# The first folds of a gated feed-forward kernel: factors in two halves, folds ahead of the first product, one low part moved to GpSimd

## What is computed

```python
xn = layernorm(x)                                   # over the 512 columns
def lora_linear(x, w, a, b):                        # a has rank 16
    return x @ w.T + (x @ a.T) @ b.T * 2.0
h = silu(lora_linear(xn, w1, A1, B1)) * lora_linear(xn, w3, A3, B3)    # 1376 hidden units
g = silu(lora_linear(h, w2, A2, B2))
s = causal_convolution(xn, K) + D * xn              # K: an S4 kernel of 512 taps
out = x + s * g
```

## Time and profile before

| | us |
|---|---|
| median of 3 runs (406.47 to 406.7) | 406.63 |
| the profiled execution | 406.52 |
| its span in the trace | 404.7 |
| TensorE busy in the span | 399.2 (99%) |
| VectorE busy | 207.4 (51%) |
| ScalarE busy | 111.5 (28%) |
| GpSimd busy | 80.3 (20%) |

### The profile page before, as it was taken

The page is one execution under the profiler, slowest core; times in us unless marked ns, Lnnn a source line. Parts: engine busy times, 40 slices in busy tenths (PEclk is TensorE's granted clock), DMA queues, the critical chain, the costliest instruction groups (busy, mean ns, idle before and its releaser), DMA issues.

```text
span 404.7 us, 5106 instructions
## 1 busy us (share of the span) xinstructions
PE 399.2 (99%) x1838; PEld 332.9 (82%) x1838; DVE 207.4 (51%) x323; ACT 111.5 (28%) x185; POOL 80.3 (20%) x141
## 2 busy tenths in 40 slices
PE   8999999999999999999999999999999999999996
PEld 7988888888888888888888888888888888888885
DVE  5877776794883336553345236754236134411227
ACT  7554232222541111222232112222123111211122
POOL 6686745403510113300000101600000000000000
PEclk9999999999999999999999999999999999999999
DMA  8583743614325102000005301000002000000002
GB/s 275 147 218 97 230 149 110 209 41 126 110 89 173 52 2 52 2 1 0 2 1 193 118 0 52 0 0 0 0 0 104 2 0 0 2 0 0 2 0 104
DMA packets 14515, 26.90 MB, mean 66 GB/s; under 512 B 2816, under 2 KB 4576, under 8 KB 14368
## 3 DMA queue, kind: packets, MB, share of 16 engines
q1 hardware_dynamic: 13488, 24.53, 19.1%
q0 software_dynamic: 720, 1.60, 1.5%
q10 hardware_dynamic: 288, 0.52, 0.3%
HBM read 21.45 MB, written 4.54 MB: 64 GB/s over the span
## 4 chain that ended last, share of the span: by engine, by line
PE 95%; DVE 1%; DMA 1%; ACT 1%; issue 1%; POOL 0%; DVEq 0%; ACTq 0%; POOLq 0%
PE h L1173 19%; PE h L1175 19%; PE h L1174 19%; PE f L1173 10%; PE f L1175 10%; PE f L1174 10%; PE h L1196 2%; PE spare L1160 1%; PE spare L1175 1%; PE spare L1173 1%; PE spare L1174 1%; DMA xn<-x_dram 1%; PE spare L1155 1%; DVE xres L946 0%; ACT xn L723 0%
## 5 line engine op out<-in xcount | busy, mean ns | idle before, releaser
L1173 PE MATMUL h<-xt,w 128*128 (+2 forms) x340 | 131.3, 386 | 0.0
L1174 PE MATMUL h<-xt,w 128*128 (+2 forms) x340 | 131.2, 386 | 0.0
L1175 PE MATMUL h<-xt,w 128*128 (+2 forms) x340 | 131.1, 386 | 0.0
L913 DVE TENSOR_TENSOR ghl<-g,ghl 128x512 fp32r<-128x512 f32 x44 | 31.7, 721 | 83.5 <-ACT ghl L715 83.5
L1173 PEld LDWEIGHTS h<-xt,w 128*128 128x128 f32 x340 | 63.9, 188 | 12.8 <-DVE w L852 0.3
L1175 PEld LDWEIGHTS h<-xt,w 128*128 128x128 f32 x340 | 63.9, 188 | 12.8
L1174 PEld LDWEIGHTS h<-xt,w 128*128 128x128 f32 x340 | 63.9, 188 | 12.6
L1173 PE MATMUL f<-ghl,w2f 128*128 128x512 f32 x176 | 68.7, 390 | 0.0
L1174 PE MATMUL f<-ghl,w2f 128*128 128x512 f32 x176 | 68.6, 390 | 0.0
L1175 PE MATMUL f<-ghl,w2f 128*128 128x512 f32 x176 | 68.5, 389 | 0.0
L908 DVE TENSOR_TENSOR g<-g,h 128x512 f32<-128x512 f32 x40 | 27.5, 688 | 77.3 <-PE h L1175 77.2
(11 more groups left out here) (187 smaller groups left out, 353.0 us busy)
## 6 DMA issues: line engine op xcount, KB each, us to landing
raw<-w_dram SPq DMA_DIRECT2D x28, 256.0 KB, 4.0
outT_dram<-xres SPq DMA_DIRECT2D x15, 256.0 KB, 2.4
xres<-xT_dram SPq DMA_DIRECT2D x3, 1024.0 KB, 6.0
rows_next<-x_dram SPq DMA_DIRECT2D x4, 512.0 KB, 3.6
scale_rows<-scales_scratch SPq DMA_DIRECT2D x3, 512.0 KB, 4.1
rows<-x_dram SPq DMA_DIRECT2D x2, 512.0 KB, 6.5
dft_sb<-dft_dram SPq DMA_DIRECT2D x1, 1024.0 KB, 5.0
xres<-xT_dram SPq DMA_DIRECT2D x4, 256.0 KB, 3.9
```

The costliest lines, as they stand in the source:

```text
L913: nc.vector.tensor_tensor(ghl[:, 1, :], g[:, :], ghl[:, 0, :].bitcast(F32), ALU.subtract).then_inc(glo_done, 1)
L1173: pe.matmul(out, w[1], m[0], start=start, stop=False)
L1174: pe.matmul(out, w[0], m[1], start=False, stop=False)
L1175: return pe.matmul(out, w[0], m[0], start=False, stop=stop)
```

## The change

The factors are laid out anew (A1, B1, A3, B3) and loaded in two halves of 768 columns, each as soon as its own half is cleared; the first half is all that the folds of w1 need. The constants `lane_c`, which hold the identity for the transposes, are issued from ScalarE's list in place of SP's. TensorE multiplies cleared data 8 times in place of 11, then folds all four tiles before its first real product, and the first products come in another order. VectorE adds the first two folds one row tile earlier each, and no longer makes the low part of (1, 0): GpSimd does, after its third row scale and ahead of its fourth. ScalarE copies the second transposed tile before it scales the third.

```diff
-FIRST_COLS = {1: 2 * D, 3: 2 * D + 2 * P}
+FIRST_COLS = {1: D, 3: 2 * D + 2 * P}
-FACTORS_BY_DVE = 832
+FACTORS = LORA_FIRST // 2
-A_FIRST = {1: 0, 3: D}
+A_FIRST = {1: 0, 3: D + 2 * P}
-POOL_LO = [(1, 3), (3, 3), (3, 4)]
+POOL_LO = [(1, 0), (1, 3), (3, 3), (3, 4)]
...
-            sync.wait_ge(factors_dve, 1)
-            sync.wait_ge(factors_pool, 1)
-            sync.dma_start(lr[0:P:STACK_STEP, :], lora).then_inc(lora_in, 16)
-            sync.dma_start(lane_c[:, :], lanes).then_inc(const_in, 16)
+            for i in range(2):
+                sync.wait_ge(factors_dve, i + 1)
+                sync.wait_ge(factors_pool, i + 1)
+                cols = slice(i * FACTORS, (i + 1) * FACTORS)
+                sync.dma_start(lr[0:P:STACK_STEP, cols], lora[:, cols]).then_inc(lora_in[i], 16)
...
+            act.dma_start(lane_c[:, :], lanes).then_inc(const_in, 16)
             act.wait_ge(g_cleared, 1)
...
             fold_hi(1, 0)
             rows_hi(0)
+            rows_hi(1)
             rows_norm(2)
-            rows_hi(1)
             spread_cast(spread_in, slice(0, LANES_EARLY))
+            fold_hi(3, 0)
             rows_norm(3)
-            fold_hi(3, 0)
...
+                def part(out, kind, w, m, cols, start, stop):
+                    for c in range(DC):
+                        mm = pe.matmul(out[:, cols], w13_tile(kind, 0, w)[:, c, :], xt[:, 0, m, c, cols],
+                                       start=(start and c == 0), stop=(stop and c == DC - 1))
+                    return mm
+
                 pe.wait_ge(g_cleared, 1)
-                keep_busy(11)
-                pe.wait_ge(lora_in, 16)
+                keep_busy(8)
+                pe.wait_ge(lora_in[0], 16)
                 fold(1, 0)
+                pe.wait_ge(lora_in[1], 16)
                 fold(3, 0)
...
+            for i in range(2):
+                nc.gpsimd.memset(lr[:, i * FACTORS + FACTORS // 2:(i + 1) * FACTORS], 0.0).then_inc(factors_pool, 1)
...
                 pool.wait_ge(first_shift, r + 1)
+                if r == 2:
+                    fold_lo(1, 0)
```

More of the change, by code:

```diff
@@ L404, in build @@
         raw_in = [sem(f"raw_in{i}") for i in range(6)]
-        lora_in, const_in = sem("lora_in"), sem("const_in")
+        lora_in, const_in = [sem(f"lora_in{i}") for i in range(2)], sem("const_in")
         spread_in, late_in, stack_cleared = sem("spread_in"), sem("late_in"), sem("stack_cleared")
@@ L1216, in start @@
                 turn_rows(0)
+                fold(1, 1)
                 turn_rows(1)
-                fold(1, 1)
-                turn_rows(2)
+                fold(3, 1)
                 pe.wait_ge(whi_done, 1)
                 pe.wait_ge(xhi_done, RT // 2)
-                for c in range(DC):
-                    pe.matmul(h1[:, lo], w13_tile(1, 0, 0)[:, c, :], xt[:, 0, 0, c, lo], start=(c == 0), stop=False)
-                fold(3, 1)
-                turn_rows(3)
-                wait_split(pe, 1, 0)
-                pe.wait_ge(xlo_done, RT // 2)
-                for c in range(DC):
-                    pe.matmul(h1[:, lo], w13_tile(1, 0, 1)[:, c, :], xt[:, 0, 0, c, lo], start=False, stop=False)
-                    pe.matmul(h1[:, lo], w13_tile(1, 0, 0)[:, c, :], xt[:, 0, 1, c, lo], start=False, stop=(c == DC - 1))
+                part(h1, 1, 0, 0, lo, True, False)
+                turn_rows(2)
+                pe.wait_ge(xlo_done, RT // 2)
+                part(h1, 1, 0, 1, lo, False, False)
+                wait_split(pe, 1, 0)
+                part(h1, 1, 1, 0, lo, False, True)
+                turn_rows(3)
+                pe.wait_ge(whi_done, 2)
+                part(h3, 3, 0, 0, lo, True, False)
+                part(h3, 3, 0, 1, lo, False, False)
                 wait_split(pe, 3, 0)
-                hidden(0, 0, 0, 3, h3, lo)
+                part(h3, 3, 1, 0, lo, False, True)
+                pe.wait_ge(xhi_done, RT)
+                part(h1, 1, 0, 0, hi, True, False)
+                part(h1, 1, 1, 0, hi, False, False)
                 pe.wait_ge(xlo_done, RT)
-                hidden(0, 0, 0, 1, h1, hi).then_inc(h1_ready, 1)
+                part(h1, 1, 0, 1, hi, False, True).then_inc(h1_ready, 1)
                 hidden(0, 0, 0, 3, h3, hi).then_inc(h3_ready, 1)
@@ L1499, in _ @@
             tt(mag[:, :], mag[:, :], res[:, :], ALU.add).then_inc(mag_ready, 1)
-            for kind, j in POOL_LO:
+            for kind, j in POOL_LO[1:]:
                 fold_lo(kind, j)
@@ L1636 @@
         "w1": c(turned_tiles(L0_ffn_w1)), "w3": c(turned_tiles(_np.asarray(L0_ffn_w3)[up])), "w2": c(_np.asarray(L0_ffn_w2).T),
-        "lora": _np.concatenate([a1, a3, b1.T[:, :2 * P], b3.T[:, :2 * P]], axis=1),
+        "lora": _np.concatenate([a1, b1.T[:, :2 * P], a3, b3.T[:, :2 * P]], axis=1),
         "lora_early": _np.concatenate([spread_out(a) for a in lora_early], axis=1),
```

22 lines of the change are left out of this document (11 added, 11 removed).

## The result

The changed kernel takes 407.90 us in the median of ten runs (407.45 to 408.41), the kernel before 406.66 (406.45 to 406.86) beside it: a ratio of 1.0029, with a 95% interval of 1.0021 to 1.0037. The profiled execution of the changed kernel took 407.78 us, 1.26 more than that of before, with a span of 405.9 us.

A forecast was written before the change was run, and what follows sets the result against it. TensorE, busy from 12.3 to 398 us, bounds the kernel, so only tile 1's start counts: 1 us of products taken forward cancels a last transpose 1.05 us later; +0.1 us on 406.52 gives 406.6 us, range 405.9 to 407.4.

The forecast's parts named there:

- I add 0.1 us for that, between nothing and 0.5.: Fourth row tile's scale on GpSimd: allowance of 0.1 us for VectorE subtracting from SBUF at the same time.
- The first fold starts at 4.95 us: TensorE's first fold: factors' first half issued at about 1.45 us, landing 3.5 us later; before, the fold started at 5.47.
- starts at 6.2: VectorE's first add: needs the fold bank (6.0 us) and the raw tile (5.8), so it starts at 6.2 us.
- the second rival: Raw tile of (1, 0) lands at 6.9 us, first add and end move by 0.7 us: 407.3 us; chance 0.14.
- GpSimd's piece, 9.4 to 11.0 us: Low part of (1, 0) on GpSimd, ahead of the fourth row tile's scale: 1.62 us, the mean of three earlier pieces.
- The first rival: GpSimd's piece does not bind: last transpose at 12.25 us, tile 1 at 17.0, time 405.9 us; chance 0.19.
- the wait for the second `rows_lo`: TensorE, after the third transpose: waits until 11.5 us, then eight products to 12.45.
- The gate activation of tile 0: Before tile 1's product: done at 17.03 us in the kernel before, forecast to move by about 0.55 to 17.6 and still fit.
- Wrong altogether would be a wait of TensorE behind 18 us that was not there before.: Sign in the changed kernel's profile that would refute the forecast; it held that whatever moves tile 1 moves the end equally.
- TensorE still slow, 0.10: Third rival: TensorE still at its slow level at the first fold, 1.8 us for 0.9: 407.5 us or more; chance 0.10.

The follow-up runs named there:

- the two single executions: The changed kernel with no edit, profiled two more times, one run each: 407.70 and 407.71 us.
- 8 pairs: Kernel before with 8 idle multiplications (16 records) in place of 11, all else as before: 406.93 us, ratio 1.0012.
- old order of the adds: Changed kernel with VectorE's two early adds put back behind the third and fourth row tile: 406.92 us with 8 idle multiplications, 406.68 us with 11.

## Why the prediction was wrong

**"I add 0.1 us for that, between nothing and 0.5."** This is the step that failed. The sentence before it has the mechanism: where both engines subtract, the later waits for the other, with 1.53 us for 0.68 in the earlier trace rows. I priced it as if it could meet only the piece of 1.62 us, whose own delay would be short. It met the smallest operation of the chain, 0.27 us long, and cost 0.8 us (1.08 less 0.27), since two VectorE operations stood back to back and GpSimd came in only after both: its operation ended 0.05 us behind the second. All 0.8 lie on the path, for ScalarE, the transpose and 36 products stand behind it. The right bounds were in my own numbers: I had the subtractions from 11.4 to 12.5 and the last scale from 11.1 to 12.0, an overlap, and the most that it could cost is the length of both subtractions, 1.1 us. That GpSimd would not get in between the two, no row of the kernel before had shown. The Trainium skill (SBUF — State Buffer, section "Who interferes with whom") says that a VectorE instruction with two SBUF inputs contends with a GpSimd instruction that reads SBUF, that the lock on their shared ports is exclusive, and that issue order, not op shape, decides who blocks. The traces agree: with VectorE 0.05 us ahead GpSimd's 0.27 us became 1.08 (11.73 and 11.78 us), and with GpSimd 0.05 us ahead VectorE's 0.69 became 1.80 (101.26 and 101.31 us).

**"The first fold starts at 4.95 us"; the first add "starts at 6.2".** They came at 5.30 and 6.58 us. The issue was at 1.51 as said (1.45), but the half of 48 KB took 3.7 us to land where the whole of 96 KB had taken 3.6. Halving the bytes bought nothing of the landing; the earlier fold is the earlier issue alone, 0.27 us of which 0.17 arrived. The add's delay went on microsecond for microsecond, as the second rival says, though it had blamed the raw tile: fourth row tile at 9.40 for 9.02, last scale at 11.13 for 11.1 only because of the next point. This term was mis-sized by 0.38 us, and of the two misses it is the smaller.

**GpSimd's piece, 9.4 to 11.0 us.** It ran from 9.78 and took 1.28 us, the lower bound, not 1.62. Of the three of the earlier trace rows two had a subtraction of VectorE's from SBUF ahead of them and took 1.75 and 1.81 us (the second is the longest, not the 1.75 that the prediction named); the third had only one of VectorE's adds beside it, whose other input is in a fold bank, and took 1.30. This one had none either. So the mean of the three was no price of an undisturbed piece, and 1.28 us is 1.9 times VectorE's 0.68, near the factor of two that the prediction set aside. That gave 0.34 us back. The first rival did not come true even so: the last scale could have started at 9.40 + 1.35 = 10.75 us and stood behind the piece until 11.13. The sum of the three terms is +0.8 (collision) + 0.38 - 0.34 less the 0.1 allowed, 0.74 us, and the last transpose stood at 13.76 in place of 13.0.

**TensorE.** First transpose 7.29 (7.1), second 8.65 (8.45), the wait for the second `rows_lo` until 11.87 (11.5): right but for the late add. From the last transpose to tile 1 it took 4.81 us (18.57 less 13.76), against 4.7: the 36 products were counted right, and so was the trade of 8 products against the later transpose. The gate activation of tile 0 came at 17.84 (17.6) and still fitted, but for 0.08 us at most: tile 1's second product follows its first after 0.31 us, in the kernel before after 0.23.

**"Wrong altogether would be a wait of TensorE behind 18 us that was not there before."** There is one, the 0.35 us at 105.52. It carries 0.26 us of the profiled execution's 1.26; in the two single executions 0.01 and 0.32 us went late, the 0.32 by the wait at 110.99. This the prediction had at nothing: it let whatever moves tile 1 move the end by as much.

**TensorE still slow, 0.10.** In the four traces of the changed kernel the folds ran at the fast pace, so this rival isn't what made its profile slow. But it is real: with 8 pairs (kernel before, and old order of the adds) 9 of 22 runs lie above 407.6 us, where none of the 25 of the kernel before on that chip does; with 11 pairs, over all chips, it is 12 of 117 (105 of the kernel before, 12 of the old order), eight of them on the one chip where 8 pairs made no difference. How much rarer it is with 11 is therefore not settled. That the upper runs are late rises is shown where they were profiled (408.51 us, and 409.20, of which nearly half is a late loss), and is an inference for the others. The prediction said that by a moving moment of the rise it can happen in some runs, as the Trainium skill has it (TensorE: Matmul & The Clock Gate, section "What's actually happening"), and then set that aside because three runs agreed within 0.23 us. Those three were of a kernel with 22 idle records; they could not speak for one with 16. How many of the changed kernel's own runs are of this kind stays open: five of ten took 408.0 to 408.4 us, above every one of the three profiled with the collision (407.70 to 407.78), and none of those five has a trace.

What also stays open is why nine of twelve runs fell in the upper group when GpSimd's piece was back on VectorE, where the kernel before with as many idle multiplications had four of eleven.

## What to carry to other kernels

When work is moved to GpSimd, look not at how long the moved piece takes but at which small GpSimd operation now stands beside VectorE's subtractions from SBUF: it can cost the whole run of them, on the path, and in the trace an added wait on VectorE of 0.27 us was worth 0.75 us to TensorE. An order that loads the same engines with more slack (the first add behind a row tile) is worth more than an earlier start, since what varies from run to run, a landing or the clock's rise, then stays hidden. And a profile with a thin margin should be taken more than once: the changed kernel gave 407.7 three times and 406.99 once, and the pair explained it.

## What the runs showed of the hardware

- An operation of GpSimd on 128x1 values took 0.27 us alone and 1.07 or 1.08 beside two VectorE subtractions of 0.48 and 0.68 us, in four traces of this study (three with 8 pairs, one with 11). GpSimd did not get in between the two VectorE instructions, which follow each other closely; VectorE did get in between two GpSimd operations of 128x512, 1.14 to 1.16 us after the first had started, in eleven traces.
- Whether TensorE had risen when the folds started is told by the spacing of its records, 3.72 to 3.79 us against 2.05 for 16, and not by the granted clock, which the rows give as 1.00 in both. After 10 idle records and 1.72 us of waiting it had not; after 16 it had in seven traces of nine; after 22 it came within the first two folds at the latest (2.05 to 2.54 us for their 16 records) in all eight, but in five of them the idle records themselves had run slowly for longer (5.06 or 5.07 us in place of 4.2 to 4.4), and the folds started at 5.85 or 5.86 us.
- The first transfer of 48 KB landed no earlier than one of 96 KB (3.7 and 3.6 us). A 320 KB transfer took 6.6 us to land issued 0.73 us behind one of 512 KB, and 4.5 us where 2.46 lay between them.
- GpSimd's 128x512 float32 subtraction took 1.28 to 1.30 us alone or beside a VectorE add with one input in SBUF, and 1.75 and 1.81 us behind a VectorE subtraction from SBUF.
